# Weighing a strip's values in two halves a slot apart, and making a block's strip keys and queries five slots earlier

## The reference, cut to what matters

```python
x = x + conv(group_norm(x))      # neighbourhood attention: 16 heads of 8, each pixel looks at 7 x 7 keys
t = tokens(x)                    # 3136 tokens of 128 channels
t = t + attn(ln(t))              # 8 heads of 16, every token looks at all 3136
t = t + ffn(ln(t))               # two 128 x 128 products, one dequantised from 4 bits
```

```python
l = einsum('bhijd,bhijd->bhij', q, k_shifted) + bias      # for each of 49 shifts
attn = softmax(stack(l), axis=-1)
out = sum(attn[..., t, None] * v_shifted[t])              # "values" below
y = out @ proj_w.T + proj_b
```

## Time and profile before

| | us |
|---|---|
| median of 3 runs | 9278.91 (9278.07 to 9288.71) |
| the profiled execution | 9294.23 |
| its span, first to last instruction | 9292.4 |

### The profile page before, as it was taken

How to read it: one execution, slowest core, us unless ns; L and a number is a source line. 1 busy time by engine, 2 the same in 40 slices (tenths; PEclk the granted TensorE clock), 3 DMA queues, 4 the chain that set the end, 5 groups by cost and what they waited for, 6 DMA issues and landing times.

```text
span 9292.4 us, 432513 instructions
## 1 busy us (share of the span) xinstructions
PE 8644.9 (93%) x173512; PEld 4571.7 (49%) x173512; DVE 7385.2 (79%) x12442; ACT 6737.1 (73%) x14241; POOL 2839.5 (31%) x2805
## 2 busy tenths in 40 slices
PE   5789999999999999999999999999999999999998
PEld 4445554555445554455544555545545455444443
DVE  5577878888788887878878887788877888788985
ACT  2367777777777777777777777777777777778877
POOL 5514441244302443034430343304433044320000
PEclk8899999999999999999999999999999999999999
DMA  1120101101011010110101100020011201011000
GB/s 44 35 53 20 26 22 41 30 20 26 25 42 26 21 28 24 43 27 18 28 24 49 24 19 25 24 55 17 22 27 27 45 17 25 25 28 30 9 10 9
DMA packets 312339, 257.30 MB, mean 28 GB/s; under 512 B 97244, under 2 KB 303052, under 8 KB 308300
## 3 DMA queue, kind: packets, MB, share of 16 engines
q1 hardware_dynamic: 310348, 229.05, 10.1%
HBM read 136.82 MB, written 78.05 MB: 23 GB/s over the span
## 4 chain that ended last, share of the span: by engine, by line
PE 84%; issue 6%; DVE 4%; ACT 3%; POOL 2%; DMA 1%; SPq 0%; ACTq 0%; DVEq 0%; POOLq 0%
PE PS L1240 22%; PE PS L1172 22%; PE PS L1225 20%; PE PS L978 6%; PE PS L1036 5%; PE PS L1044 4%; PE PS L1054 2%; DVE block_max L1704 1%; ACT PB L1456 1%; PE PS L1028 1%; ACT tail L1374 1%; PE PS L1084 0%; PE PS L1010 0%; DVE NM L1581 0%; DMA vT_padded<-SC 0%
## 5 line engine op out<-in xcount | busy, mean ns | idle before, releaser
L1704 DVE TENSOR_REDUCE block_max<-PS 128x1 f32<-128x512 f32 (+1 forms) x9632 | 6134.7, 683 | 1214.7 <-PE PS L1172 1139.3
L1456 ACT ACTIVATE PB<-PS 128x448 f32<-128x448 f32 (+1 forms) x11200 | 5459.0, 545 | 1599.3 <-PE PS L1225 1573.7
L1225 PE MATMUL PS<-QP,KP 99*32 99x448 bf16 x43904 | 4320.5, 355 | 82.6 <-ACT PB L1456 52.3
L1172 PE MATMUL PS<-KP,QP 96*32 96x512 bf16 (+1 forms) x43904 | 4011.9, 356 | 91.5 <-issue 79.9
L1240 PE MATMUL PS<-PB,VA 128*32 128x448 f32 x22400 | 2720.7, 541 | 26.4 <-issue 25.8
L1225 PEld LDWEIGHTS PS<-QP,KP 99*32 99x32 bf16 x43904 | 1415.1, 97 | 1290.0 <-issue 466.6
L1172 PEld LDWEIGHTS PS<-KP,QP 96*32 96x32 bf16 x43904 | 1283.3, 96 | 1507.4 <-issue 587.8
L1240 PEld LDWEIGHTS PS<-PB,VA 128*32 128x32 f32 x22400 | 787.1, 111 | 421.4 <-issue 51.9
L884 POOL TENSOR_TENSOR SC<-SC,NM 128x1120 f32<-128x1120 f32 x210 | 433.1, 2063 | 1826.7 <-DVE NM L1581 1826.6
L858 POOL TENSOR_TENSOR QB<-Qn,C 128x896 f32<-128x896 f32 x392 | 662.0, 1709 | 12.0 <-ACT Qn L1314 12.0
L1036 PE MATMUL PS<-KR,QB 128*32 128x80 f32 x21952 | 553.7, 234 | 82.3 <-DVE VS L1620 22.2
(11 more groups left out here) (114 smaller groups left out, 4717.6 us busy)
## 6 DMA issues: line engine op xcount, KB each, us to landing
QP<-q_dram SPq DMA_DIRECT2D x672, 56.0 KB, 2.1
VP<-vT_padded SPq DMA_DIRECT2D x448, 70.0 KB
k_dram<-k_parts SPq DMA_DIRECT2D x56, 336.0 KB, 2.9
KP<-k_dram SPq DMA_DIRECT2D x336, 56.0 KB, 2.1
q_dram<-q_parts SPq DMA_DIRECT2D x56, 336.0 KB, 2.5
KP<-k_dram SPq DMA_DIRECT2D x48, 392.0 KB, 6.4
VA<-v_dram SPq DMA_DIRECT2D x16, 816.0 KB, 4.3
vT_padded<-SC SPq DMA_DIRECT2D x112, 112.0 KB
```

Source lines behind the costliest of these rows:

```text
L1172: ins = mm(PS[at:at + QT, bank, n * width:(n + 1) * width], QP[0:ROWS, Q_SLOTS[k % AUNITS], t:t + QT], KP[0:ROWS, g, t // BLK, keys], star ...
L1225: ins = mm(PS[k0:k0 + 32, bank, 0:BLK], KP[0:ROWSM, k // NBLK, h, c * P + k0:c * P + k0 + 32], QP[0:ROWSM, Q_SLOTS[k], h * BLK:(h + 1) * B ...
L1456: S.activation(exp_buffer(k, c)[0:n, h, :], PS[0:n, at % ST_BANKS, 0:BLK], ACT.Exp, scale=float(ADIM) ** -0.5).then_inc(exp_done, 1)
L1704: V.tensor_reduce(block_max[:, k % 2, queries.start:queries.stop, j], tile, AX.X, ALU.max).then_inc(max_read, 1)
```

## The change

The values of a strip can be weighed by two tasks. `early_values` does units 0 to 6 at (t + 16, 0) if the place (t + 16, 1) is not taken; that place is then kept free. The task at (t + 17, 0) is still listed as `values`; PE's `beside` does `late_values`, units 7 to 13, in its place when the previous side task was `early_values`, with no wait. The two waits of `values` (on `turned_read` and on `windows_in`) go to `early_values`. The bank is read once, as before, after the second half. Where (t + 16, 1) is taken, `values` stays whole.

Worked out from the plan: 23 of the 28 strips of an image are split; strips 19, 20, 22, 24 and 25 stay whole. That makes 161 split strips in the seven images with an ahead part. The start `alone` is as it was.

`norm`, `k1` and `q1` of blocks 1 to 6 start five slots earlier. The table gives the places:

| block | k1 before | k1 after | q1 before | q1 after |
|---|---|---|---|---|
| 1 | 49, 1 | 44, 0 | 50, 1 | 44, 1 |
| 2 | 86, 1 | 80, 1 | 88, 1 | 81, 1 |
| 3 | 123, 1 | 116, 1 | 125, 1 | 117, 1 |
| 4 | 158, 1 | 152, 1 | 160, 1 | 155, 1 |
| 5 | 194, 1 | 188, 1 | 197, 1 | 189, 1 |
| 6 | 234, 1 | 224, 1 | 235, 0 | 225, 1 |

Because places are now taken or kept, `q2` and `v2` of blocks 0 to 3 and `k2` of block 1 come one or two slots later, with their splits and stores (for block 2, `q2` from (163, 0) to (164, 1) and `v2` from (164, 1) to (165, 1)).

```diff
@@ class Plan
     def place(self, t, task, i):
         sub = 0
-        while (t, sub) in self.taken:
+        while (t, sub) in self.taken or (t, sub) in self.kept:
             t, sub = t + sub, 1 - sub
...
-            self.fix(t + 2 * PERIOD - 1, 0, "values", s)
+            u = t + 2 * PERIOD - 2
+            if (u, 1) not in self.taken:
+                self.fix(u, 0, "early_values", s)
+                self.kept.add((u, 1))
+            self.fix(u + 1, 0, "values", s)
...
-            t = FIRST_STRIP + (PERIOD * (BLOCK_STRIPS * j - 3) if j else -7)
+            t = FIRST_STRIP + (PERIOD * (BLOCK_STRIPS * j - 3) - 5 if j else -7)
             self.fix(t, 1, "norm", NBLK + j)
             t = self.place(t + 1, "k1", j)
             self.place(t, "q1", j)
@@ TensorE
+                def weighed(units, bank):
+                    for u in units:
+                        for g in range(4):
+                            ins = mm(PS[32 * g:32 * g + 32, bank, 32 * u:32 * u + 32],
+                                     VP[0:KPAD, u, 32 * g:32 * g + 32], PT[0:KPAD, u, 32 * g:32 * g + 32],
+                                     start=True, stop=True, tile_position=(0, 32 * g))
+                    return ins
+
+                def early_values(s, bank):
+                    pe.wait_ge(turned_read, of(b, ahead, 4 * STRIPS, 4 * s + 4))
+                    pe.wait_ge(windows_in[s % 2], of(b, ahead, 16 * windows_loaded(STRIPS - 2 + s % 2), 16 * windows_loaded(s)))
+                    apart(pe)
+                    weighed(range(UNITS // 2), bank)
+
+                def late_values(bank):
+                    weighed(range(UNITS // 2, UNITS), bank).then_inc(pv_in, 1)
...
                 def beside(t, sub):
                     if (t, sub) in plan.taken:
-                        pe.wait_ge(*side_read(b, 1, *previous[0]))
-                        apart(pe)
-                        do(*plan.taken[t, sub], SIDE_BANK)
+                        if previous[0][0] == "early_values":
+                            do("late_values", previous[0][1], SIDE_BANK)
+                        else:
+                            pe.wait_ge(*side_read(b, 1, *previous[0]))
+                            apart(pe)
+                            do(*plan.taken[t, sub], SIDE_BANK)
                         previous[0] = plan.taken[t, sub]
```

More of the change, by code:

```diff
@@ L96 @@
 SIDE_READER = {"gn_mean": "dve", "gn_var": "act", "k1": "dve", "v1": "act", "q1": "act", "scores": "dve",
-               "turn": "act", "values": "act", "proj": "dve", "mean2": "dve", "var2": "act", "k2": "act",
+               "turn": "act", "values": "act", "early_values": "act", "proj": "dve", "mean2": "dve", "var2": "act", "k2": "act",
                "q2": "act", "v2": "dve", "spread": "act", "project": "dve", "mean3": "dve", "var3": "act",
@@ L104, in __init__ @@
     def __init__(self, front, attention):
-        self.at, self.taken = collections.defaultdict(list), {}
+        self.at, self.taken, self.kept = collections.defaultdict(list), {}, set()
         if attention:
@@ L1051, in values @@
                     apart(pe)
-                    for u in range(UNITS):
-                        for g in range(4):
-                            ins = mm(PS[32 * g:32 * g + 32, bank, 32 * u:32 * u + 32],
-                                     VP[0:KPAD, u, 32 * g:32 * g + 32], PT[0:KPAD, u, 32 * g:32 * g + 32],
-                                     start=True, stop=True, tile_position=(0, 32 * g))
-                    ins.then_inc(pv_in, 1)
+                    weighed(range(UNITS), bank).then_inc(pv_in, 1)
                 def proj(j, bank):
@@ L1129, in do @@
                         turn(i // 4, i % 4, bank)
+                    elif task == "early_values":
+                        early_values(i, bank)
+                    elif task == "late_values":
+                        late_values(bank)
                     elif task == "values":
```

## The result

The changed kernel takes 9195.29 us (median of 4 runs, 9191.61 to 9206.65), the kernel before 9279.86 in the 4 runs beside it: a ratio of 0.9913, with a 95% interval of 0.9901 to 0.9926. That is faster by 84.6 us; forecast were 9184 and 95. One execution of the changed kernel, in its second measurement further down, ran at a granted clock of 0.747 and took 11113.58 us; it is left out of every time given. The profiled execution is 9206.65 us with a span of 9204.8, so it is 87.6 us shorter than the profiled one of before. In the changed kernel the numbers of the lines have moved: `values` is L1055 (was L1054), `turn` L1048, the scores L1248, the maxima tiles L1192, `weigh` L1263, the copy of `roll_keys` L838, `spread_queries` L862, `halve_sum` L869, the read of `k1` L1585 and of `q1` L1337, `norm` L1579.

What follows compares the result with a forecast made beforehand. The prediction took PE, busy for 93%, to bound the kernel. Its terms, 47 + 4 + 44 + 0 = 95 us, taken off 9278.9 gave 9184 us, with a range of 9125 to 9250.

Steps and rivals of the forecast that it cites:

- the second term: Splitting values into halves gives back PE's instruction-supply stalls in the split slot pairs: 44 us gained.
- Slot 236: Pair of slots 235 and 236: earlier keys end PE's wait behind POOL's roll, 47 us gained, bounds 33 to 64.
- Waits for `q1`: Side tasks waiting for ACT's read of q1: one wait fewer an image, 4 us gained, between 4 lost and 8 gained.
- `norm` of block 1: DVE's norm, half a slot ahead of k1 at (44, 0): priced at nothing, up to 1 us x 7 if late.
- Stalls given back: Split pairs, slots t + 16 and t + 17: two thirds of PE's empty time recovered, 44 us, bounds 0 to 99.
- the 3 named as a sign: Expected sign in the trace: empty PE in the 23 split pairs down from 10 to near 3 us an image.
- The sign of being wrong: Clean pairs growing beyond 6.2 us, or "issue" gaps as often behind the halves or in slots of scores.
- The halves' own cost: Slots with values: two halves lengthen them as much as one whole, no change; between 166 us lost and 40 gained.
- rival D: Each half costs PE a fixed entry, 2 x 0.95 us in place of 0.87: 9350 us, chance 0.05.
- B: The split gives back nothing, since stalls move or block supply is not what PE waits for: 9228 us, chance 0.20.
- C: The k1 move fails, since DVE's norm and POOL's roll wait elsewhere or POOL is late anyhow: 9235 us, chance 0.07.
- The mixture: Cancelling mixture of B, C and a mild form of rival D: 9260 to 9297 us, chance 0.05.

Runs made afterwards that it cites:

- the keys alone: Kernel before with only the keys and queries of blocks 1 to 6 five slots earlier, values whole: 9229.67 us, ratio 0.993.
- the halves alone: Changed kernel with keys and queries back at their old places, so only the split of values remains: 9230.95 us, ratio 0.9935.
- the doubled values: Kernel before with the values of strips 6, 7, 9, 14 and 18 weighed twice in a row: 9433.43 us, against 9286.88 beside it.
- the one with halves: Kernel before plus halves, POOL's two strip 22 tasks two slots later, strip 10 whole: 9181.11 us; with 120 more first-image instructions 9193.29 us.

## Why the prediction was right

It named both causes, and the sum was 10 us too high. That the second term came out so near is in part luck. Step by step:

- **Slot 236, 47 us** (33 to 64): 45.6 measured. That POOL's roll was the root is shown by the run that moves only POOL's two tasks: 40.4 us in the same pair. The pair of strip 4 was a good model: 8.23 taken, 8.45 found (59.13 / 7), since 1.18 us of the wait for `ffn`'s read stays.
- **Waits for `q1`, 4 us**: right in sign, but too small, and outside the bound of 8: 19.2 us in 34 waits are 7.0 in 14, so 12.2 less. What stayed comes from the other half of the change: first halves that stand where no side task stood. With the keys alone none is left.
- **`norm` of block 1, priced at nothing, up to 7**: it costs 4.9 us. PE's waits for `norm` at `k1` are 6.6 us in 8 times where one of 1.7 was. DVE's queue in the fourth image shows it, with PE's line below: `norm` comes up behind five reductions for the maxima, ends at 3974.02, and `k1` begins at 3974.07.

```profile
3969.88 3.07 DVE L1727 TENSOR_REDUCE block_max<-PS 128x1 f32<-128x512 f32 x5
3972.87 1.15 DVE L1579 TENSOR_SCALAR XN<-X,gn 128x448 f32<-128x448 f32 x1
...
3974.07 0.96 PE L982 MATMUL PS<-XN,W_qkv 128*32 128x448 f32 x8 [0.69 <-DVE XN L1579]
```

- **Stalls given back, 44 us** (0 to 99): 54.9 by span for the halves alone; in the changed kernel's split pairs 42.2 in six images and 5.7 in the first, 47.9. The size is right by errors that cancel. The mechanism, less empty PE, gave 65.1 - 40.1 = 25.0 us in six images and 5.71 - 4.12 = 1.6 in the first, 26.6 in all. The gaps put down to "issue" did fall by 29.1 of 47.6, near the two thirds of the forecast, but the forecast took all empty PE of the pairs for such gaps. The eight stalled strips keep 20.7 / 6 = 3.4 us of empty PE an image, where 3.3 follow from its two thirds. But the other fifteen catch 19.4 - 7.9 = 11.5 us in six images; "clean pairs may catch a small stall" was said, and was not taken off. So the 23 pairs have 6.7 us of empty PE an image, not the 3 named as a sign. The other 21.3 us of the 47.9 are less busy PE (848.50 to 831.32, and 139.10 to 135.01 in the first image), and most of that is moved work: `v2` of blocks 0, 2 and 3 has left the pairs of strips 4, 12 and 16, whose 18 windows go from 137.81 to 121.62 us of busy PE. It is done in other slots now; outside the split pairs, the pair 235/236 and slot 227 PE's busy time grows by 11 us in the seven images.
- **The sign of being wrong**: "if clean pairs grow beyond 6.2 us". Two of the nine did, 6.33 and 7.22, by waits for the bank and by a moved `q1`, and not by gaps in the supply. With the halves alone strip 7 takes 5.60 and strip 11 6.48. What the sign stood for, stalls that only move to other places, did not come: ahead of the weighing, for one, PE's gaps put down to "issue" fall from 25.8 us in 26 times to 6.8 in 8.
- **The halves' own cost, 0**: right; 204.93 to 202.69 us in the 36 pairs that kept their neighbours. A half adds 0.47 and 0.25 us to its slot, so rival D (2 x 0.95) is out.
- **Not in the sum**: slot 227, 5.7 us, where the early `k1` and `q1` now stand in front of a whole `values`; and slot 145, 19.5 us in seven images by its own (34.88 - 15.38), a collision of the first half with the narrow tiles. It lies in a split pair, so it is already taken off the 47.9. I had looked at what stood in the side places, and not at what PE's main work is in the 20th chunk of a unit.

The seven images then add up: 45.6 + 47.9 - 5.7 = 87.8, less 2.5 us elsewhere, gives 85.3. In those 2.5 stand `v2` and the 4.9 at `norm` as losses, and the waits for `q1` and the slots that `k1` and `q1` left as gains.

Of the rivals, B (the split gives nothing) is refuted by the halves alone. The Trainium skill's "Runtime: NRT & Kernel Launch", section "Instruction fetch mechanics", on which it leaned, has the next block fetched during the present one, so that the crossing is mostly hidden. Here the 2.01 us in slot 145 and the 12.3 us of the doubled values are not hidden. Most crossings are, as the rule says: 1393 packets of q8 start from the first slot of the kernel before on, against the 79 gaps. C is refuted by the pair 235/236. The mixture did not occur.

What stays open: that it is the place of a block's border that lengthens slot 227 is read from the traces and not tested; why slot 36, which holds no burst of `values`, has 3.0 to 5.5 us of empty PE in three of the middle images before and none in the other three; and how much of the 0.16 us of an increment is its own cost. No experiment tried the halves at another cut than 7 and 7, nor a split strip 19 over two slots.

## What to carry to other kernels

A gap inside a run of equal instructions with no engine to blame was here a gap in the supply of instructions, and the records of the instruction queue's packets show it: lay the gaps beside them, count instructions per microsecond, and spread the densest burst over the slots beside it. A whole slot apart helped here, and half a slot did not. Look in both slots at the main work as well as at the side tasks; another burst there undoes it. Where an engine's queue is in order, a task that waits for its producer should not stand ahead of a task that others need sooner: in the pair 235/236 moving two consumers on POOL gave 40 of the 46 us that moving the keys and queries of six blocks gave, and it left slot 227 as it was (32.1 us in seven images, 32.3 before).

## What the runs showed of the hardware

- An increment of a semaphore on PE's queue costs about 0.16 us when 120 stand in a row: slots 40 and 41 went from 5.85 to 24.90 us.
- In 78 of 79 gaps put down to "issue" PE went on 2.1 to 3.4 us after a packet of its instruction queue began, half of them within 2.5 us. The packets of that queue take 1.1 us each (median).
- What the end of the loop's body takes depends on where the stream's blocks are cut. Slot 349 and, before it, slot 36 of the fourth image, before and with 120 instructions more in the first image only (slot 36 is the first row of each fence, slot 349 the second):

```profile
3986.20:3991.91 5.71, 2.67 (x44) 1.08 (x37) 2.70 (x5) 2.45 (x5) 0.00 (x0) 1.00 0.27 40
5010.18:5022.09 11.91, 2.53 (x33) 1.16 (x29) 2.32 (x4) 2.41 (x5) 0.00 (x0) 0.78 0.52 151
```

```profile
4012.46:4014.85 2.39, 2.39 (x44) 1.09 (x40) 2.19 (x5) 1.90 (x4) 0.00 (x0) 1.00 0.85 118
5044.65:5050.13 5.48, 2.37 (x33) 0.94 (x28) 2.33 (x4) 2.40 (x5) 0.00 (x0) 1.00 0.36 104
```

  9.4 us of empty PE are 3.1, and 3.0 are none. (Slot 36 has 3.0 to 5.5 us in three middle images of the kernel before, and none in any image of the three runs with 120 instructions more in the first image.) In the kernel before that gain is more than eaten by the pairs that stall anew and by the added instructions; in the one with halves it pays for them (ratios of 0.989 and 0.9891).
- TensorE's clock has two levels, 1.2 and 2.4 GHz. In slot 145 of the changed kernel the granted share was 1.00 in the images with 1.75 us of empty PE or less; it was 0.79 and 0.77 in the third and fifth with 2.01 us and 0.74 in the seventh with 2.29, but 1.00 in the sixth with 4.98 - 2.96 = 2.02 us. So the length of the gap alone doesn't decide. What a drop costs shows in the earlier trace rows and above: the 112 matmuls take 1.72 in place of 1.15 us.
